# First stage of a four-stage sequence kernel: the block loop unrolled and skewed by one block, with the vector work regrouped

## The reference

```
xn = layernorm(x)                    # per row
a, k, v, q, g = xn @ Wa, xn @ Wk, xn @ Wv, xn @ Wq, xn @ Wg
# a is complex (real half, imaginary half); as the kernel has it:
#   decay = sigmoid(|a|), angle = arg(a) summed along the sequence
h[t] = gate(a[t]) * h[t-1] + k[t] * v[t]        # associative_scan
y = q * h                            # then a group norm over the sequence
```

## Time and profile before

| what | us |
|---|---|
| median of 3 runs | 3300.76 (3300.14 to 3303.49) |
| the profiled execution | 3283.15 |
| its span in the trace | 3281.4 |
| first stage, from the span's start to VectorE's last instruction | 392.0 |
| VectorE busy in the 8 blocks, 30.43 to 391.98 us | 339.06 |
| TensorE, ScalarE busy in the same stretch | 191.39, 164.20 |

### The profile page before, as it was taken

The page is one execution under the profiler, slowest core; times in us unless marked ns, Lnnn a source line. Parts: engine busy times, 40 slices in busy tenths (PEclk is TensorE's granted clock), DMA queues, the critical chain, the costliest instruction groups (busy, mean ns, idle before and its releaser), DMA issues. The chain is left out here.

```text
span 3281.4 us, 36485 instructions
## 1 busy us (share of the span) xinstructions
PE 2640.8 (80%) x12168; PEld 1810.6 (55%) x12202; DVE 1978.0 (60%) x3556; ACT 1056.0 (32%) x1645; POOL 1380.4 (42%) x865
## 2 busy tenths in 40 slices
PE   6555389957799999999467888888889676997998
PEld 2222156636699999999123333433334334665997
DVE  8999867645112122211699999999899994332211
ACT  4544212210111111111345546455465430221111
POOL 0000034417333333333048687696886951112332
PEclk8777689975899999999688999989989887998999
DMA  3000100001799999987400000100100100115996
GB/s 110 0 0 0 43 8 13 19 27 34 260 324 322 324 326 327 323 309 250 139 19 33 33 33 26 39 33 26 39 26 34 37 27 26 39 39 214 346 348 239
DMA packets 95173, 395.04 MB, mean 120 GB/s; under 512 B 21366, under 2 KB 48518, under 8 KB 72544
## 3 DMA queue, kind: packets, MB, share of 16 engines
q1 hardware_dynamic: 73472, 351.46, 30.5%
q0 software_dynamic: 21600, 42.37, 3.6%
HBM read 364.94 MB, written 39.29 MB: 123 GB/s over the span
## 5 line engine op out<-in xcount | busy, mean ns | idle before, releaser
L1246 POOL TENSOR_TENSOR ss_h<-ss_h,ss_cs 128x2048 f32<-128x2048 f32 x128 | 578.9, 4525 | 78.3 <-DVE ss_h L1612 70.4
L1326 PE MATMUL ss_y<-ss_h,all_ident 128*128 128x512 f32 x1024 | 520.8, 657 | 67.6 <-POOL ss_h L1246 62.0
L1095 DVE TENSOR_TENSOR experts_in<-experts_sil,experts_pU 128x512 f32<-128x512 f32 x176 | 121.2, 689 | 637.3 <-PE experts_pU L1039 637.3
L1612 DVE TENSOR_TENSOR_SCAN ss_h<-ss_da,ss_c_h,ss_dbu 128x512 f32<-128x512 f32 x384 | 470.8, 1268 | 7.1 <-ACT ss_da L1472 0.3
L1326 PEld LDWEIGHTS ss_y<-ss_h,all_ident 128*128 128x128 f32 x1024 | 213.3, 212 | 334.0 <-issue 259.0
L1472 ACT ACTIVATE ss_da<-ss_dt,ss_decay 128x512 f32<-128x512 f32 x512 | 326.7, 711 | 119.6 <-DVE ss_h L1612 64.4
L1605 DVE TENSOR_TENSOR ss_dbu<-ss_dtx,ss_bB 128x1024 f32<-128x1024 f32 x256 | 314.6, 1229 | 61.2 <-PE ss_bB L1316 26.7
L1039 PE MATMUL experts_pG<-experts_xt,experts_wa 128*128 128x128 f32 x2816 | 346.7, 277 | 2.2 <-DMA experts_wa<-in_w_all 2.1
L1039 PE MATMUL experts_pU<-experts_xt,experts_wa 128*128 128x128 f32 x2816 | 343.2, 275 | 0.0
L1039 PEld LDWEIGHTS experts_pG<-experts_xt,experts_wa 128*128 128x128 f32 x2816 | 331.5, 193 | 3.6 <-ACT experts_xt L1065 2.7
L1048 PE MATMUL experts_pY<-experts_wa,experts_in 128*128 128x256 f32 x1408 | 332.7, 379 | 0.0
(11 more groups left out here) (322 smaller groups left out, 3733.8 us busy)
## 6 DMA issues: line engine op xcount, KB each, us to landing
experts_wa<-in_w_all SPq DMA_DIRECT2D x176, 1536.0 KB, 9.0
ss_cs<-ss_c_rows SPq DMA_DIRECT2D x64, 512.0 KB, 3.5
moe_rows<-route_xn SPq DMA_DIRECT2D x16, 512.0 KB, 3.1
ss_h<-moe_ys SPq DMA_DIRECT2D x5, 1024.0 KB, 7.9
all_x<-in_x SPq DMA_DIRECT2D x8, 512.0 KB, 9.3
gf_xb<-in_x SPq DMA_DIRECT2D x8, 512.0 KB, 3.7
moe_rows<-all_x SPq DMA_DIRECT2D x8, 512.0 KB, 3.0
experts_xr<-moe_rows,moe_token POOLq DMA_INDIRECT x176, 7.5
```

What stands on the lines that cost most here:

```text
L1095: nc.vector.tensor_tensor(IN[t.two][:].rearrange("p f t -> p (f t)"), SIL[t.two][:], pU[t.two][:], ALU.mult)\
L1246: pool.tensor_tensor(h[:], h[:], CS[q % 2][:, n % GROUP].unsqueeze(1).to_broadcast([P, CI, BT]), ALU.mult)\
L1326: mm = pe.matmul(y[:, c], ident[:], H[(b * N + n) % RING][:, c], start=(n == 0), stop=(n == N - 1))
L1612: ins = V.tensor_tensor_scan(H[(b * N + n) % RING][:, c], DA[(b * N + n) % AHEAD][:, c], DBU[:, c % 2], first, ALU.mult, ALU.add)
```

## The change

The three loops are written out block by block, and VectorE and ScalarE work on two blocks at once. In step i VectorE does the half tangent of block i, the states of block i-1, the phase of block i, K times V and squared length of block i+1, and the outputs of block i-1. K V, Q, decay, sine and cosine therefore have two buffers each. Q is multiplied onto the states before the rotation back. Since the rotation keeps lengths, the sum of the two squares is taken from these products, by ScalarE, which writes the squares into `pT`. The sum of the imaginary part is taken as two sums added at the end. Further:

- The normalisation moves from VectorE to ScalarE, in place in `XN`; the copy L227 goes.
- The sign's scaling moves to ScalarE (`magnitude`); the real part is copied with its sign to SBUF, the sign test reads it there, and |real part| is taken later from that copy. So ScalarE, not VectorE, frees the banks of the real part.
- Carried values are read from the last column of the block before (0 at a sequence's start), without small copies.
- ScalarE does the roots of block i+1 at the end of step i, after the copies of Q and G; for block 0 they stand ahead of the copies of K and Q.

The diff, with the declarations cut, and the lines of the old bodies left out (they stand above):

```diff
+        rstd, tmp, shift = m_.sb("rstd", [P, NT]), m_.sb("tmp", [P, NT]), m_.sb("shift", [P, NT])
+        SQR, SQI, AIM, ARS, KS, NEG, SGN, PHI, WR, E1, E2, UR, UI = (
+            m_.sb(n, [P, KD, BT]) for n in ("sqr", "sqi", "aim", "ars", "ks", "neg", "sgn", "phi", "wr", "e1", "e2", "ur", "ui"))
+        two = lambda name: [m_.sb(f"{name}{h}", [P, KD, BT]) for h in range(2)]
+        KV, QS, A, SN, CS = two("kv"), two("qs"), two("a"), two("sn"), two("cs")
+        stats = KS[:, 0, 0:NT * 6].rearrange("p (t s) -> p t s", s=6)
+        MAG, TAN = SQR, SQI
...
+                    wait(pe, "xt_done", i * KD)
+                    wait(pe, "squared", (i - 2) * KD * 2)
                     for j in range(TPB):
                         for c in range(KD):
-                            mm = pe.transpose(pT[:, c, j * P:(j + 1) * P], XNB[:, j, c * P:(c + 1) * P], ident[:])
+                            mm = pe.transpose(pT[:, c, j * P:(j + 1) * P], XN[:, i * TPB + j, c * P:(c + 1) * P], ident[:])
                     mm.then_inc(s["xt_raw"], 1)
...
-                with pe.Fori(0, NB - 1) as i:
+                pe.wait_ge(s["w_loaded"], 16)
+                for i in range(NB):
                     project(i)
-                    turn(i + 1)
-                project(NB - 1)
+                    if i < NB - 1:
+                        turn(i + 1)
...
+                def normalise(i):
+                    act.wait_ge(s["stats_ready"], 1 if i == 0 else 2)
+                    for t in range(i * TPB, (i + 1) * TPB):
+                        A_(XN[:, t], XN[:, t], ACT.Identity, scale=rstd[:, t:t + 1], bias=shift[:, t:t + 1]).then_inc(s["xn_done"], 1)
...
+                def squares(i):
+                    wait(act, "t_done", i * KD)
+                    wait(act, "atan_done", i * KD)
+                    wait(act, "a_done", i * KD)
                     for c in range(KD):
                         act.wait_ge(proj[AR], i * KD + (c + 1))
                         A_(SQR[:, c], bank_of(AR, c), ACT.Square)
+                        A_(ARS[:, c], bank_of(AR, c), ACT.Copy).then_inc(free_of(AR, c), 1)
                         act.wait_ge(proj[AI_], i * KD + (c + 1))
                         A_(SQI[:, c], bank_of(AI_, c), ACT.Square).then_inc(s["sq_done"], 1)
                         A_(AIM[:, c], bank_of(AI_, c), ACT.Copy).then_inc(free_of(AI_, c), 1)
+                def copy_k(i):
+                    act.wait_ge(s["stats_ready"], 2)
+                    wait(act, "t_done", i * KD)
+                    wait(act, "y_done", (i - 2) * KD)
                     for c in range(KD):
                         act.wait_ge(proj[K_], i * KD + (c + 1))
+                        if i > 0:
+                            wait_freed(act, i - 1, V_, c)
                         A_(KS[:, c], bank_of(K_, c), ACT.Copy).then_inc(free_of(K_, c), 1)
+                def copy_q(i):
+                    wait(act, "u_done", (i - 1) * KD)
+                    for c in range(KD):
+                        act.wait_ge(proj[Q_], i * KD + (c + 1))
+                        A_(QS[i % 2][:, c], bank_of(Q_, c), ACT.Copy).then_inc(free_of(Q_, c), 1)
+                        act.wait_ge(proj[G_], i * KD + (c + 1))
+                        A_(SG[:, c, i * BT:(i + 1) * BT], bank_of(G_, c), ACT.Silu).then_inc(free_of(G_, c), 1)
+                def magnitude(i):
+                    wait(act, "turn_done", i * KD)
+                    for c in range(KD):
+                        act.wait_ge(s["neg_done"], i * KD + (c + 1))
+                        A_(SGN[:, c], NEG[:, c], ACT.Copy, scale=-4.0 / math.pi, bias=1.0 / math.pi).then_inc(s["sgn_done"], 1)
+                        A_(ARS[:, c], ARS[:, c], ACT.Abs)
                     for c in range(KD):
                         act.wait_ge(s["m2_done"], i * KD + (c + 1))
                         A_(MAG[:, c], SQR[:, c], ACT.Sqrt).then_inc(s["mag_done"], 1)
+                def decay(i):
+                    wait(act, "u_done", (i - 1) * KD)
                     for c in range(KD):
                         act.wait_ge(s["mag_done"], i * KD + (c + 1))
+                        A_(A[i % 2][:, c], MAG[:, c], ACT.Sigmoid).then_inc(s["a_done"], 1)
+                def angle(i):
+                    wait(act, "trig_done", i * KD)
                     for c in range(KD):
                         act.wait_ge(s["t_done"], i * KD + (c + 1))
                         A_(PHI[:, c], TAN[:, c], ACT.Arctan).then_inc(s["atan_done"], 1)
+                def rotation(i):
+                    wait(act, "y_done", (i - 1) * KD)
                     for c in range(KD):
                         act.wait_ge(s["turn_done"], i * KD + (c + 1))
+                        A_(PHI[:, c], WR[:, c], ACT.Abs).then_inc(s["abs_done"], 1)
+                        A_(SN[i % 2][:, c], WR[:, c], ACT.Sin, scale=TURN)
                         act.wait_ge(s["abs_done"], i * KD + (c + 1))
+                        A_(CS[i % 2][:, c], PHI[:, c], ACT.Sin, scale=-TURN, bias=quarter[:]).then_inc(s["trig_done"], 1)
+                def sum_squares(i):
+                    act.wait_ge(s["xt_done"], min(i + 3, NB) * KD)
+                    for c in range(KD):
+                        act.wait_ge(s["u_done"], i * KD + (c + 1))
+                        for n, src in ((2, E1), (3, E2)):
+                            wait(act, "squared", (i * KD + c) * 2 + n - 3)
+                            A_(pT[:, n - 2], src[:, c], ACT.Square, accum_out=sum_at(i, c, n)).then_inc(s["squared"], 1)
+                normalise(0)
+                copy_xt(0)
+                squares(0)
+                magnitude(0)
+                copy_k(0)
+                normalise(1)
+                copy_q(0)
+                for i in range(NB + 1):
+                    more = i < NB - 1
+                    if i < NB:
+                        decay(i)
                     if more:
                         copy_xt(i + 1)
+                    if i < NB - 2:
+                        normalise(i + 2)
+                    if i < NB:
+                        angle(i)
+                    if more:
+                        squares(i + 1)
+                        copy_k(i + 1)
+                    if i > 0:
+                        sum_squares(i - 1)
+                    if i < NB:
+                        rotation(i)
+                    if more:
+                        copy_q(i + 1)
+                        magnitude(i + 1)
...
+                def kv_products(i):
+                    for c in range(KD):
+                        dve.wait_ge(proj[V_], i * KD + (c + 1))
+                        wait_freed(dve, i, K_, c)
+                        V.tensor_tensor(KV[i % 2][:, c], KS[:, c], bank_of(V_, c), ALU.mult).then_inc(free_of(V_, c), 1)
+                def squared_length(i):
                     for c in range(KD):
                         dve.wait_ge(s["sq_done"], i * KD + (c + 1))
                         V.tensor_tensor(SQR[:, c], SQR[:, c], SQI[:, c], ALU.add).then_inc(s["m2_done"], 1)
+                        V.tensor_scalar(NEG[:, c], ARS[:, c], 0.0, 0.5, ALU.is_lt, ALU.mult).then_inc(s["neg_done"], 1)
+                def half_tangent(i):
+                    wait_freed(dve, i, AI_, 1)
+                    for c in range(KD):
+                        wait_freed(dve, i, V_, c)
+                    for c in range(KD):
+                        dve.wait_ge(s["mag_done"], i * KD + (c + 1))
+                        ch.link(V.scalar_tensor_tensor(KS[:, c], ARS[:, c], 1e-30, MAG[:, c], ALU.add, ALU.add))
+                        ch.link(V.reciprocal(TAN[:, c], KS[:, c]))
+                        V.tensor_tensor(TAN[:, c], AIM[:, c], TAN[:, c], ALU.mult).then_inc(s["t_done"], 1)
+                        dve.wait_ge(s["t_done"], i * KD + (c + 1))
+                def phase(i):
+                    dve.wait_ge(s["sgn_done"], i * KD + KD)
+                    wait(dve, "trig_done", i * KD)
+                    for c in range(KD):
+                        dve.wait_ge(s["atan_done"], i * KD + (c + 1))
+                        ch.link(V.tensor_tensor(PHI[:, c], PHI[:, c], SGN[:, c], ALU.mult))
+                        first = 0.0 if starts_at(i) else WR[:, c, BT - 1:BT]
+                        ch.link(V.tensor_tensor_scan(PHI[:, c], PHI[:, c], NEG[:, c], first, ALU.add, ALU.add))
+                        ch.link(V.tensor_scalar(WR[:, c], PHI[:, c], ROUND, ROUND, ALU.add, ALU.subtract))
+                        V.tensor_tensor(WR[:, c], PHI[:, c], WR[:, c], ALU.subtract).then_inc(s["turn_done"], 1)
+                        dve.wait_ge(s["turn_done"], i * KD + (c + 1))
+                def states(i):
+                    kv, qs, a, sn, cs = (b[i % 2] for b in (KV, QS, A, SN, CS))
+                    for c in range(KD):
+                        wait_freed(dve, i, V_, c)
+                        dve.wait_ge(s["trig_done"], i * KD + (c + 1))
+                        wait(dve, "squared", i * KD * 2)
+                        wait(dve, "y_done", i * KD)
```

(45 more changed lines are left out.)

134 lines of the change are left out of this document (24 added, 110 removed).

## The result

| | us |
|---|---|
| changed kernel, median of 4 runs | 3244.03 (3240.97 to 3246.25) |
| kernel before, median of 4 runs | 3301.24 (3300.14 to 3303.49) |
| ratio, with its 95% interval | 0.9823 (0.9811 to 0.9836) |
| profiled execution of the changed kernel, its span | 3244.09, 3242.3 |
| first stage, last vector instruction ends: before, after | 391.98, 335.32 |

The change takes 57.2 us off; 3248 were forecast, with a range of 3234 to 3266. The first stage ends 56.7 us earlier. The next stage's first vector instruction follows 3.70 us behind instead of 3.29, so 56.3 us of the gain are left there.

The account below looks back on a forecast made before the run. VectorE's list was taken as the bound: terms of 36.02 plus 0.4 give 36.4 us a block against 45.7; the first stage ends 52.3 us earlier, so from the median 3300.76 the forecast was 3248 us, range 3234 to 3266.

Parts of the forecast that it names:

- states: VectorE, per block: four products 2.40 and 0.12 wait, four scans 4.66 and 0.04 wait, four Q products 2.40: 9.62 us.
- outputs: VectorE, per block: two halves of 0.60 + 0.72 + 0.83 + 0.62 + 0.83, 7.20 us.
- allowance: VectorE's block: 0.4 us, between 0 and 1.5, for more semaphore waits, all on constants; brings 36.02 to 36.4.
- The sum: First stage: from 70.9, six steps of 36.4 to 289.3, seventh to 322.6, last to 339.7 us; 52.3 less.
- The fill: First stage's start: root of block 1 there at 70.9 us, needed at 53.2, so VectorE idles 17.7 us.
- Rival 3: First stage's start shorter, or waits on constants cheaper: six us off and 0.4 a block, 3239 us; chance 0.15.
- The root: ScalarE has the next block's first root at T + 9.2 (T: a phase's end), 1.1 us in hand before VectorE asks.
- The table switch: ScalarE's change of function table: 1.40 us by the trace, against 2.66 us by the Trainium skill's page.
- Rival 2: ScalarE's switch of table costs about one load (1.28) more: root 2.6 us late in six steps, 3268 us; chance 0.02.
- Where the 9.3 come from: VectorE's saving per block, 45.7 to 36.4 us, itemised: among others normalisation 1.4, squares of the sums 2.8, remaining products 1.3.
- the cover that ends ScalarE's 100 us of waiting without a wait on VectorE: States between half tangent and phase: arctangents done before the phase asks at T + 29.6 (T: end of a phase).
- Rival 4: Parts of two blocks wait for each other at a ring bank or buffer, losing half the gain: 3274 us; chance 0.04.

Follow-up runs that it names:

- the two kernels with padding: Changed kernel with two or six copies of 128x512, each waited for, ahead of the roots on ScalarE: 3248.04 and 3269.73 us.

## Why the prediction was right

**The bound.** VectorE's list in steps was the right reading: 97.6% busy, steps of 35.6 to 35.9 against 36.4. Two of the prediction's own signs were missed narrowly, by the same terms: steps of 36 to 37 us, and an end at 336 to 344 us. Term by term, for the step from 142.26 to 178.14:

| term | forecast | measured |
|---|---|---|
| half tangent | 9.66 | 9.68 |
| states | 9.62 | 9.86 |
| phase | 6.46 | 6.46 |
| K times V | 1.20 | 1.20 |
| squared length, sign test | 1.88 | 1.88 |
| outputs | 7.20 | 6.80 |
| allowance | 0.4 | 0 |
| sum | 36.4 | 35.88 |

Two terms were off in size. *Outputs*: four waits behind an accumulated sum were put at 0.83 from a row that stood in a loop; written out they take 0.73 or 0.74. That is also why the allowance of 0.4 was not needed: it was put in for waits that in fact became cheaper. *States*: the pair of scans was priced by 2.33 from the third stage, whose row names no column as a start value, as the rows here do. The states of block 0, which start from 0 and not from a column, show what that is worth:
```profile
82.95 1.22 DVE L409 TENSOR_TENSOR_SCAN gl_ur<-gl_a,gl_e 128x512 f32<-128x512 f32 x1
84.09 1.20 DVE L409 TENSOR_TENSOR_SCAN gl_ui<-gl_a,gl_e 128x512 f32<-128x512 f32 x1
...
87.62 0.69 DVE L413 TENSOR_TENSOR gl_e<-gl_qs,gl_ur 128x512 f32<-128x512 f32 x1
```
Without a start column the four scans and the wait take 4.67 (82.95 to 87.62), as forecast; with one they take 4.91 (154.47 to 159.38). The difference is the 0.24 by which the states were short. The sign test out of SBUF is 0.34, as taken from its neighbour.

**The sum.** From 70.73, six steps end at 285.4 (forecast 289.3), and the rest takes 49.9 (50.4): 335.3 against 339.7. The 4.4 us are 3.7 from the steps' price, 0.5 from the tail, 0.2 from the fill. The total was 4 us too high for this reason. (The fill's terms as the prediction lists them, 66.5 + 0.5 + 2.1 + 2.0, add to 71.1, not 70.9; that is too little to matter.)

**The fill** came out by its own chain: 43.41 for 43.3, 57.42 for 57.7, 69.97 + 0.6 = 70.6 for 70.9, idle 17.8 for 17.7. The pace of TensorE's products was 22.56 / 12 = 1.88 us for 1.93, at a granted clock of 0.92 over them. The 0.74 that the prediction looked at is a mean over the stage before with its idle times; over the 44 matmuls of the earlier trace rows it was 0.90, which is why the pace hardly changed. That the fill agrees to 0.2 us is in part luck: in four of the other kernels the same products took 20.86 us, and started up to 1.4 us later. Rival 3 had hoped for six us from the clock; the most that any execution shows is 1.7 us over the one measured, and of that rival only the cheaper waits came here.

**The root.** Forecast 1.1 us in hand, found 0.7, and the two kernels with padding confirm it. ScalarE was as forecast (first root at 177.4, T + 9.1 from T = 168.26, for T + 9.2); it was VectorE that asked earlier, because its outputs were cheaper. A margin between two engines shrinks when the slower of them gets faster.

**The table switch** costs 64.54 - 62.65 - 0.49 = 1.40 us again in the new order, as in the earlier trace rows, and 176.76 - 174.82 - 0.52 = 1.42 ahead of the root. The Trainium skill (ScalarE: Activation LUTs, What ACT_TABLE_LOAD costs) gives about 1283 ns for the load, which the 1.28 of the rows match, and 1380 ns of drain beside it, which no row here shows. Rival 2 falls.

**Where the text said less than it should.** "Where the 9.3 come from" left the loops as a saving out, though they are 1.5 of the 9.8. And the prediction called the states "the cover that ends ScalarE's 100 us of waiting without a wait on VectorE". The kernel without the skew shows that this cover is worth 1.8 us a block. ScalarE's waits for the half tangent are 33.1 us there and 32.1 with the skew, and it is busy for the same 167.3 of 245 us in both, where it was busy for 112.0 before: what ended the 100 us is the shorter list of VectorE and the longer one of ScalarE. The prediction priced the fill, but did not set it against what the skew saves; the two cancel.

**Rival 4** fell with the waits: none of VectorE's for TensorE or ScalarE lies behind the fill. Its force shows in the kernel with one decay buffer.

## What to carry to other kernels

Where one engine is busy over 90% of a stage, count its list in steps from start to start, entry by entry, and check the other engines' lists only for the one answer that comes last; the margin there is worth nothing until it is gone, and then counts fully in every step. A skew pays its fill once and earns the covered wait per block: with eight blocks, 1.8 us covered in each later one and 17.8 us of fill, it only broke even, and its first step deserves an order of its own. Before a software pipeline is credited with a gain, run it without the skew; and look first for the buffers that an engine writes ahead of its reader: with one copy of the decay, everything queued behind ScalarE's wait for it stood still. A fill that hangs on TensorE's pace differs by 1 to 2 us from one execution to the next, so judge small edits by the step.
